# Output stores of the steady blocks issued by ScalarE instead of SyncE

## The reference

```
feats   = 1/sqrt(512) * exp(xis) * exp(x @ (xis[:,None]*proj).T - 0.5*|x|^2*xis^2)
weights = the same function of input_weights
x = layernorm(x + feats @ weights.T)
real, imag = x @ cos(theta + theta_noise),  x @ sin(phi + phi_noise)
x = layernorm(x + sqrt(real^2 + imag^2))
```

## Time and profile before

| | us |
|---|---|
| median of 3 runs (692.81 to 693.67) | 693.6 |
| the profiled execution's own time | 692.88 |
| span of the profiled execution | 691.1 |
| busy in it: PE / DVE / ACT / POOL | 681.6 / 579.5 / 482.8 / 170.7 |

### The profile page before, as it was taken

One profiled execution on the slowest core, in us unless ns is written; L12 is line 12 of the kernel. 1 busy time (PEld: TensorE's weight loads), 2 busy tenths in 40 slices (PEclk: granted clock), 3 DMA queues, 4 the chain that ended last, 5 costly groups with the idle time before them and its releaser, 6 DMA issues.

```text
span 691.1 us, 10093 instructions
## 1 busy us (share of the span) xinstructions
PE 681.6 (99%) x3010; PEld 562.9 (81%) x3010; DVE 579.5 (84%) x903; ACT 482.8 (70%) x771; POOL 170.7 (25%) x240
## 2 busy tenths in 40 slices
PE   9999999999999999999999999999999999999995
PEld 8888888888888888888888888888888888888874
DVE  6788899888879798887969878797887979888877
ACT  6867998386585758668585776858667685866466
POOL 5772304103012040301304031130302104030205
PEclk9999999999999999999999999999999999999998
DMA  8862031471835538083653817456281654707142
GB/s 311 236 138 61 16 115 69 107 213 27 215 96 122 181 79 238 18 188 127 125 182 70 223 40 162 142 127 192 42 218 74 146 157 108 211 24 176 31 121 92
DMA packets 179302, 90.23 MB, mean 131 GB/s; under 512 B 121040, under 2 KB 149712, under 8 KB 179280
## 3 DMA queue, kind: packets, MB, share of 16 engines
q1 hardware_dynamic: 175328, 86.30, 46.4%
q0 software_dynamic: 1152, 2.10, 1.8%
q10 hardware_dynamic: 2800, 1.57, 0.8%
HBM read 58.46 MB, written 31.49 MB: 130 GB/s over the span
## 4 chain that ended last, share of the span: by engine, by line
PE 88%; DVE 5%; issue 4%; ACT 1%; DMA 1%; POOL 0%; SPq 0%; POOLq 0%; ACTq 0%; DVEq 0%
PE token_ps L1068 7%; PE token_ps L1070 7%; PE token_ps L1069 7%; PE token_ps L1181 6%; PE token_ps L1182 6%; PE token_ps L1183 6%; PE project_ps L1012 5%; PE project_ps L1014 4%; PE project_ps L1013 4%; PE project_ps L1181 4%; PE project_ps L1182 4%; PE project_ps L1183 4%; PE turn_ps L1012 4%; PE turn_ps L1014 4%; PE turn_ps L1013 4%
## 5 line engine op out<-in xcount | busy, mean ns | idle before, releaser
L505 POOL TENSOR_TENSOR plain_late<-z,plain_late 128x1024 f32<-128x1024 f32 x13 | 31.3, 2409 | 288.0 <-ACT plain_late L754 288.0
L1068 PE MATMUL token_ps<-W_hi,F_hi 128*128 128x512 f32 x240 | 93.4, 389 | 0.0
L1069 PE MATMUL token_ps<-W_lo,F_hi 128*128 128x512 f32 x240 | 93.4, 389 | 0.0
L1070 PE MATMUL token_ps<-W_hi,F_lo 128*128 128x512 f32 x240 | 93.4, 389 | 0.0
L760 ACT ACTIVATE o_tile<-plain_late,shift,rstd 128x512 f32<-128x512 f32 x56 | 42.8, 809 | 57.7 <-POOL shift L518 50.3
L1288 DVE TENSOR_TENSOR zT_lo<-plain_zT_lo,zT_hi 128x768 fp32r<-128x768 f32 (+1 forms) x54 | 58.9, 1090 | 6.6 <-ACT zT_hi L849 5.1
L646 ACT ACTIVATE F_hi<-plain_expo,ab 128x512 fp32r<-128x512 f32 x62 | 44.5, 718 | 24.1 <-DVE plain_expo L1293 24.0
L754 ACT ACTIVATE plain_late<-plain_late 128x1024 f32<-128x1024 f32 x28 | 29.6, 1057 | 42.2 <-POOL plain_late L501 39.3
L1012 PE MATMUL project_ps<-xT_hi,gs_hi 128*128 128x512 f32 x144 | 56.7, 394 | 0.0
L1014 PE MATMUL project_ps<-xT_hi,gs_lo 128*128 128x512 f32 x144 | 56.1, 390 | 0.0
L1013 PE MATMUL project_ps<-xT_lo,gs_hi 128*128 128x512 f32 x144 | 56.1, 389 | 0.0
(11 more groups left out here) (335 smaller groups left out, 1904.1 us busy)
## 6 DMA issues: line engine op xcount, KB each, us to landing
x_tok<-in_x SPq DMA_DIRECT2D x16, 1024.0 KB, 5.9
out_tokens<-o_tile SPq DMA_DIRECT2D x62, 256.0 KB, 3.2
plain_xT_lo<-in_xT SPq DMA_DIRECT2D x14, 1024.0 KB, 8.9
turned_pair<-plain_late SPq DMA_DIRECT2D x104, 128.0 KB, 2.8
plain_zT_lo<-turned_pair SPq DMA_DIRECT2D x27, 256.0 KB, 2.8
plain_zT_lo<-turned_pair SPq DMA_DIRECT2D x54, 128.0 KB, 2.9
norm_bc<-token_norms SPq DMA_DIRECT2D x15, 256.0 KB, 3.0
z<-in_wT ACTq DMA_DIRECT2D x4, 256.0 KB, 4.9
```

Source lines behind the costliest of these rows:

```text
L1068: nc.tensor.matmul(o, F_hi[:, c, cols], W_hi[:, c, :], start=(c == 0), stop=False)
L1069: nc.tensor.matmul(o, F_hi[:, c, cols], W_lo[:, c, :], start=False, stop=False)
L1070: return nc.tensor.matmul(o, F_lo[:, c, cols], W_hi[:, c, :], start=False, stop=(c == C - 1))
```

## The change

`store_out` is defined for ACT too, and ACT's `open_step` issues the stores of tiles 0 and 1 behind both of their norms, and those of tiles 2 and 3 behind both of theirs. SP's `step` no longer issues them, and so its fetch of pair 0 stands directly behind the strips of pair 0. This holds for the stores of blocks 1 to 13 (52 tiles). The stores of block 0 (made by DVE), of block 14 and of block 15 stay where they are.

```diff
-            def step(b, slot, ahead, first=False, moved=False, behind_plain=False):
+            def step(b, slot, ahead, moved=True):
                 if moved:
                     store_squares(b, 0)
-                if behind_plain:
-
+                if moved:
                     fetch_halves(b, 0)
-                if not first:
-                    store_out(b - 1, 0)
-                    store_out(b - 1, 1)
-                if moved:
-                    if not behind_plain:
-                        fetch_halves(b, 0)
                     store_squares(b, 1)
                     fetch_halves(b, 1)
                 if ahead:
...
-                if not first:
-                    store_out(b - 1, 2)
-                    store_out(b - 1, 3)
                 if ahead:
                     store_norms(b + 3, 1 - slot)
                     fetch_norms(b + 3, 1 - slot)
...
+            def store_out(b, j):
+                act.wait_ge(out_made, C * b + j + 1)
+                act.dma_start(out_tiles[b][j], o_tile[:, j % 2, :]).then_inc(out_stored[j % 2], 16)
+
             def open_step(b, behind_plain=False, **how):
                 pair_roots(b - 1, 1)
                 norm2(b - 1, 0)
                 norm2(b - 1, 1)
+                store_out(b - 1, 0)
+                store_out(b - 1, 1)
                 load_table(ACT.Exp)
                 if behind_plain:
                     round_halves(b, 0)
                 norm2(b - 1, 2)
                 norm2(b - 1, 3)
+                store_out(b - 1, 2)
+                store_out(b - 1, 3)
```

More of the change, by code:

```diff
@@ L388, in step @@
                     fetch_norms(b + 3, 1 - slot)
-            step(0, 0, True, first=True)
+            step(0, 0, True, moved=False)
             sp.wait_ge(y_made, C * 2)
@@ L400, in _ @@
             for slot in range(2):
-                step(PLAIN + slot, slot, True, moved=True, behind_plain=(slot == 0))
+                step(PLAIN + slot, slot, True)
             with sp.Fori(2, NB // 2 - 1) as pair:
                 for slot in range(2):
-                    step(pair * 2 + slot, slot, True, moved=True)
-            step(NB - 2, 0, False, moved=True)
+                    step(pair * 2 + slot, slot, True)
+            step(NB - 2, 0, False)
             last = NB - 1
```

## The result

The changed kernel takes 717.08 us (median of 6 runs, 714.33 to 718.2) against 693.4 before: ratio 1.0338, 95% interval 1.0322 to 1.0354, so 23.7 us slower. The forecast was 696.9 with a range to 702.5. The sign and the cause (the tiles' bytes beside the strips) were forecast; the size was not, nor that PE would wait at M1 and M7 of pair 0, where the forecast had put the price at nothing.

A forecast was written before the change was run, and what follows sets the result against it. PE bounds the kernel, so only used-up slack costs. Terms: SP 0, ACT 0, late blocks 3.0 and block 2 0.3, so +3.3 us on 692.9 gives 696.2, or 696.9 against the median of 693.6; range 693.0 to 702.5.

The forecast's parts named there:

- What bounds the kernel: PE, busy 681.6 of 691.1 us, waits for nothing in a typical block; only slack of what it needs counts.
- Faster: The sign that time falls: only block 2's 0.25 us PE wait could be won, 693.3; chance 0.04 with others.
- SP, value 0: SP's queue: two store issues (1.02 us) leave, but the fetch still waits for the strips' landing; 0 us.
- ACT's issues, value 0: ACT's queue: four more issues, about 0.55 us each, hidden in idle time and under norms; 0 us.
- Rival B: ACT's queue: its issues are dear, each waiting for one of SP's; 704 us, or 699 at half; chance 0.06.
- The strips' delay: DMA engines at pair 0: tiles 0 and 1 make the strips end 1.3 us later, ends 0 and 1.5.
- The landing of the first fetch: Pair 0's fetch: its third DMA lands at 344.3 instead of 343.0; the delay just fits, price 0.
- slack of 1.38: Pair 0, typical block: 0.38 before DVE comes, 0.47 of DVE idling and 0.53 before M7 is due.
- Pair 1: Second fetch and x_tok load come 1.3 us later; costs 1.3, 1.0 and 0.7 in blocks 4, 5 and 10, sum 3.0.
- Block 2, +0.3: Block 2, where PE already waits for M7: tiles 2 and 3's issues precede the rounding; 0.3 us, ends 0 and 1.1.
- C: Second pair's tiles hit fully: delay 2.3 at the second fetch gives 708 us, 1.8 gives 702; chance 0.09.
- A: No measurable change: tiles and strips overlap in the DMA engines, delay under 1 us; 693.9 us; chance 0.36.

The follow-up runs named there:

- order experiment: The kernel before, with only SyncE's order changed: pair 0's fetch directly behind its strips, then the stores of tiles 0 and 1, all on SyncE; 720.82 us against 693.0.
- 1/16 of the bytes: The changed kernel, but each of ScalarE's 52 stores writes only 32 of 512 columns; 693.89 us against 693.49 for the kernel before.
- first experiment: Against the changed kernel, only tiles 0 and 1 stay on ScalarE; tiles 2 and 3 return to SyncE behind the loads; 712.56 us against 693.49 before.
- half of the columns: The changed kernel, but each of ScalarE's stores writes only 256 of 512 columns; 707.76 us against 693.49 for the kernel before.
- half of the rows: The changed kernel, but each of ScalarE's stores writes only the first 64 of 128 rows, full width; 702.88 us against 693.0 before.
- on one ring: The kernel before, with tiles 0 and 1 issued on SyncE between pair 0's second and third strips, block 2 in old order; 702.57 us against 693.11.
- timed stores: The changed kernel, but ScalarE stores tiles 0 and 1 after SyncE's fourth strip issue, tiles 2 and 3 before copy_W of pair 1; 693.63 us against 693.11.
- flawed one-ring kernel: The kernel before, with tiles 0 and 1 issued on SyncE between pair 0's second and third strips, block 2 included; 711.05 us against 693.0.

## Why the prediction was wrong

- **What bounds the kernel: right.** PE at its pace, slacks of about a microsecond, nothing to win. Faster was excluded rightly.
- **SP, value 0: right.** The fetch waits for the landing (4.39 us distance in the order experiment).
- **ACT's issues, value 0: right,** and by more than counted: 1/16 of the bytes costs nothing that can be measured, and the issues run under the activations. Rival B fell with it. The Trainium skill's rule on the locked descriptor generator ("Perfetto Trace Analysis", section "Per-instruction lifecycle: what the profiler-reported window actually captures") named no price; no wait for it shows on SyncE, whose four issues took 2.26 us with ScalarE's two inside them and 2.25 before.
- **The strips' delay, "I take 1.3", with 1.5 as its upper end: the step that failed.** It measured 2.29. The term took the tiles' time from a stretch in which they ran alone (347 GB/s), and added it to the strips' time. But side by side on two rings the two go worse than one after the other: 5.2 us from first to last packet against 4.4 before, where the rates of the earlier trace rows give 0.524 MB / 203 GB/s + 0.524 / 347 = 2.6 + 1.5. My upper end was an assumption of perfect sharing and no bound at all.
- **The landing of the first fetch, "now at 344.3": wrong again in the same direction.** I let tiles 2 and 3 fall on the second pair only. They were issued at 349.42, before the fetch of pair 0 at 349.64. From that fetch's start to DVE's sums it takes 4.68 us (median), and 3.93 with tiles 2 and 3 left on SyncE (first experiment). So 0.75 us more. 2.29 + 0.75 is 3.04 us of delay against the slack of 1.38 that I had worked out: 1.66 too much, and PE's waits at M1 and M7 measured 1.57 a block. The slack was right, and it holds in the other runs. DVE's sums started 8.76 us after the first strip's issue before, and 1.0 of slack was left behind them (0.47 and 0.53), so PE should wait for what goes beyond 9.76: that gives 1.03 us a block with tiles 0 and 1 alone (10.79; measured 0.88), 0.69 with half of the columns (10.45; 0.64), 0.45 with half of the rows (10.21; 0.40) and 0.30 on one ring (10.06; 0.38). In the changed kernel the 12 blocks make 18.8 of the 23.7 us. Among the due times M1 was missing, though it starves first, at 0.94 us in block 7.
- **Pair 1: delay taken as 1.3; the price of 3.0 in three late blocks.** In the change M3 and M5 cost 3.6 us in all, near the forecast by number, but for another reason: PE is late from M1 on and so gives pair 1 time. With tiles 2 and 3 alone, the second fetch came 1.6 us later and M3 of pair 0 and M5 of pair 1 cost 9.6 of 10.4 us of waits, over 0.3 us in 10 of 12 blocks and not in three.
- **Block 2, +0.3:** M1 and M7 started 0.15 and 0.33 us late, where M7 was 0.25 late before. Nearly right.
- **Rivals.** C (708, or 702 at a delay of 1.8; chance 0.09) came nearest, but I had put it on the second pair; the larger part was the first. A's argument, that strips leave data paths unused beside which tiles could slip, has its answer in the windows: 199 to 269 GB/s together while both move, where the strips alone make 203 and the tiles alone 347. The rule of the Trainium skill ("DMA: Bandwidth & Descriptors", section "Issuing engines are not separate DMA queues") holds in the runs in both halves: the DMAs interleave (978 packets of one queue and 86 of the other in the same microsecond), and the issuing engine as such is worth nothing (timed stores: 693.63). What decides is whether the tiles' bytes meet the strips and the fetch, and by that the change lost 3.4%.

The chances followed from the sum: with a slack of 1.4 us and a delay taken as 1.3 the median block came out at exactly zero. Such a near miss should have given the range above the forecast far more room than to 702.5: the 3.0 us that I had as the upper end at pair 1 lay beyond the 2.3 for which rival C's own arithmetic gave 708.

## What to carry to other kernels

A transfer that nobody waits for can still be on the critical path through the DMA engines: look at which short transfers with a waiting consumer are in flight when it starts, and count both. Moving it to another engine's queue takes away the order that one ring gave for nothing; if it has to move, tie its start to the other's issue by a semaphore, as the timed version does. And when a delay is close to a slack, price the overshoot for every block, and test with fewer bytes at the same issues: that one run told traffic from issue cost here.

## What the hardware showed beyond that

Tiles of 2 KB rows and strips of 128 B runs, 0.524 MB each: the strips' landing came 1.8 us later with the tiles within them on one ring, and 2.3 to 2.4 with the tiles on a second ring; at the 347 GB/s of the earlier trace rows the tiles take 1.5 us. ScalarE's queue issues DMAs while its activations run (0.34 us each, at 361.70 under an activation of 361.34). In the flawed one-ring kernel PE started no matmul between 142.8 and 148.51; the granted clock averaged 0.59 from 146 to 149, and it was at its lower level of 1.2 GHz (0.50) from 149 to 152, with PE back at work; the columns of these windows are as above, TensorE clock third from the end:

```profile
143.00:146.00 3.00, 0.19 (x1) 0.00 (x0) 2.83 (x7) 2.90 (x4) 0.00 (x0) 1.00 0.96 138
146.00:149.00 3.00, 0.49 (x1) 0.50 (x2) 3.00 (x7) 2.49 (x5) 0.40 (x2) 0.59 0.58 151
149.00:152.00 3.00, 3.00 (x8) 2.31 (x7) 2.97 (x7) 2.75 (x5) 0.00 (x0) 0.50 0.96 326
152.00:155.00 3.00, 3.00 (x12) 2.36 (x11) 1.84 (x3) 1.40 (x3) 0.00 (x0) 0.77 0.94 214
```

What stays open is why two rings are slower than one: the trickle at the end may come from engines that finish unevenly, but no run took the engines apart, and none gave both rings the same starting moments.
